# Scaling expert results before they are stored, and adding them to X by accumulating gathers

## The reference

```
scores = softmax(x @ gate_weight.T)              # 8 experts
topk_w, topk_idx = top_k(scores, 2)              # two experts per token, weights not renormalised
combine[t, topk_idx] = topk_w
gu  = einsum('th,efh->tef', x, gate_up_weights)
act = silu(gu[..., :F]) * gu[..., F:]            # F = 352
y   = einsum('tef,te,ehf->th', act, combine, down_weights)
y   = y + shared_ffn(x)
x   = layernorm(x + y)
```

## Time and profile before

| | us |
|---|---|
| median of 3 runs | 2266.09 |
| lowest and highest of them | 2261.15, 2271.64 |
| the profiled execution, device time | 2257.88 |
| its span in the profile, first to last instruction | 2256.1 |
| TensorE busy in the span | 1998.7 (89%) |
| VectorE busy | 1076.1 (48%) |
| ScalarE busy | 712.7 (32%) |
| GpSimd busy | 346.1 (15%) |
| expert phase, about | 1933 to 2256 |

### The profile page before, as it was taken

How to read it: one execution, slowest core, us unless ns; L and a number is a source line. 1 busy time by engine, 2 the same in 40 slices (tenths; PEclk the granted TensorE clock), 3 DMA queues, 4 the chain that set the end, 5 groups by cost and what they waited for, 6 DMA issues and landing times. The chain is left out here.

```text
span 2256.1 us, 32905 instructions
## 1 busy us (share of the span) xinstructions
PE 1998.7 (89%) x12204; PEld 1620.9 (72%) x12204; DVE 1076.1 (48%) x1877; ACT 712.7 (32%) x2272; POOL 346.1 (15%) x308
## 2 busy tenths in 40 slices
PE   5899958899999988999799997898967999899990
PEld 4767736778888857777677875676756777799990
DVE  5566743345454546433454445566765232222226
ACT  1555622334344432222131101344542121233322
POOL 1111100000000018200021100000002400544315
PEclk9999968999999999999899998899988999999995
DMA  5001124000000013000092002000013200444236
GB/s 183 18 22 39 40 105 146 32 1 1 1 1 1 1 43 112 1 0 0 27 335 86 1 1 66 1 1 1 1 42 117 112 0 0 170 164 155 82 102 196
DMA packets 61436, 135.88 MB, mean 60 GB/s; under 512 B 6256, under 2 KB 24048, under 8 KB 59376
## 3 DMA queue, kind: packets, MB, share of 16 engines
q1 hardware_dynamic: 36240, 94.14, 11.9%
q0 software_dynamic: 5840, 27.92, 3.5%
q10 hardware_dynamic: 19216, 11.89, 1.9%
HBM read 90.68 MB, written 43.25 MB: 59 GB/s over the span
## 5 line engine op out<-in xcount | busy, mean ns | idle before, releaser
L1210 PE MATMUL banks<-ternary_xth,ternary_wq 128*128 (+1 forms) x352 | 138.5, 394 | 1.4 <-DVE ternary_xtl L73 1.4
L1210 PE MATMUL banks<-ternary_xtl,ternary_wq 128*128 (+1 forms) x352 | 138.3, 393 | 0.0
L409 ACT ACTIVATE gqa_pr<-banks,gqa_nb 128x128 f32<-128x128 f32 x256 | 90.1, 379 | 60.8 <-DVE gqa_nb L545 60.8
L409 ACT ACTIVATE causal_pr<-banks,causal_nb 128x128 f32<-128x128 f32 x256 | 90.1, 378 | 56.8 <-DVE causal_nb L545 56.8
L100 PE MATMUL banks<-latent_vh,latent_cth 128*128 128x512 f32 x256 | 104.2, 407 | 3.5 <-DVE latent_ctl L923 3.5
L100 PE MATMUL banks<-weights,expert_xgh 128*128 x312 | 104.6, 335 | 2.7 <-DVE expert_xgl L1732 2.4
L101 PE MATMUL banks<-weights,expert_xgh 128*128 x312 | 101.2, 325 | 0.0
L102 PE MATMUL banks<-weights,expert_xgl 128*128 x312 | 101.1, 324 | 0.0
L102 PE MATMUL banks<-latent_vh,latent_ctl 128*128 128x512 f32 x256 | 100.1, 391 | 0.0
L101 PE MATMUL banks<-latent_vl,latent_cth 128*128 128x512 f32 x256 | 100.1, 391 | 0.0
L880 ACT ACTIVATE latent_pt<-banks 128x1024 f32<-128x1024 f32 x32 | 32.9, 1027 | 194.4 <-PE banks L1021 194.4
(11 more groups left out here) (427 smaller groups left out, 5616.1 us busy)
## 6 DMA issues: line engine op xcount, KB each, us to landing
x_slots<-decay_zeros SPq DMA_DIRECT2D x39, 256.0 KB, 3.0
y_slots<-decay_zeros SPq DMA_DIRECT2D x39, 256.0 KB, 3.3
expert_xin<-x_slots SPq DMA_DIRECT2D x39, 256.0 KB, 2.9
y_slots<-expert_ys SPq DMA_DIRECT2D x39, 256.0 KB
weights_raw<-in_expert_experts SPq DMA_DIRECT2D x4, 2176.0 KB, 8.8
gqa_tw<-in_ternary_w ACTq DMA_DIRECT2D x4, 2112.0 KB, 10.9
ternary_raw<-in_ternary_w SPq DMA_DIRECT2D x11, 768.0 KB, 4.2
expert_raw<-in_expert_experts POOLq DMA_DIRECT2D x3, 2176.0 KB, 9.5
```

The lines of the kernel that those rows point to most:

```text
L409: a = act.activation(pr[:, h, c, :], S.bank[2 * h + c // 4][:, (c % 4) * P:(c % 4 + 1) * P], ACT.Exp, bias=nb[:, h, c:c + 1], accum_out=su ...
L1210: a = pe.matmul(dst[:, :], wq[:, j, m, c * P:(c + 1) * P], x[:, c, toks], start=c == 0 and n == 0, stop=c == C - 1 and n == 1)
```

## The change

Four things are done. The decay phase zero-fills a third HBM table `s_slots`, one float per slot. GpSimd, after its 32 scatters of X in the shared phase, scatters the 32 columns of weights to `s_slots` (4 bytes per row) and waits for them. In the expert phase SyncE loads the 128 weights of each slot tile to `sc` (four buffers), and ScalarE's copy out of the bank takes them as a per-partition scale. The gathers no longer write `yg` but add to the tiles of X (`compute_op=ALU.add`); high gather t waits until low gather t has landed, low gathers wait for nothing but `landed(E - 2)`. VectorE's 32 adds are gone; its statistics wait for both gathers of a tile. All five norms stand behind all gathers on GpSimd.

```diff
@@ attention_phase, sync (decay)
-                sp.wait_ge(slots_zero, 32 * (SLOTS // P))
+                sp.dma_start(S.s_slots.rearrange("(p i) n -> p (i n)", p=P), zeros[:, 0:TILES]).then_inc(slots_zero, 16)
+                sp.wait_ge(slots_zero, 32 * (SLOTS // P) + 16)
@@ shared_ffn_phase, gpsimd (after the scatters of X)
+            for n in range(2 * B):
+                at = bass.IndirectOffsetOnAxis(ap=S.pos[:, n:n + 1], axis=0)
+                pool.indirect_dma_start(S.s_slots, at, S.score[:, n:n + 1], None).then_inc(scored, 16)
+            pool.wait_ge(scored, 16 * 2 * B)
@@ expert_ffn_phase
-    NY = 8
-        yg = S.raw[:, 0:NY * DM].rearrange("p (n d) -> p n d", d=DM)
+        sc = sb("sc", [P, NX])
@@ sync
+            def load_score(i):
+                sp.dma_start(sc[:, i % NX:i % NX + 1], rows(S.s_slots, i)).then_inc(s_in[i % NX], 16)
             for i in range(NX):
                 load(i)
+            for i in range(NX):
+                load_score(i)
...
                 sp.dma_start(rows(S.y_slots, i), ys[:, i % 2, :]).then_inc(y_out[i % 2], 16)
+                if i + NX < TILES:
+                    load_score(i + NX)
@@ gpsimd
-                pool.indirect_dma_start(yg[:, n % NY, :], None, S.y_slots, at).then_inc(yg_in[n % NY], 16)
+                pool.indirect_dma_start(S.X[:, n % B, :], None, S.y_slots, at, compute_op=ALU.add).then_inc(added[n % B], 16)
             landed(E - 2)
-            for n in range(B):
-                if n >= NY:
-                    pool.wait_ge(low_added, n - NY + 1)
-                gather(n)
+            for t in range(B):
+                gather(t)
             landed(E - 1)
             for t in range(B):
-                if t < NY:
-                    pool.wait_ge(low_added, t + NY + 1)
-                else:
-                    pool.wait_ge(high_added, t - NY + 1)
+                pool.wait_ge(added[t], 16)
                 gather(B + t)
-                if t >= NY and t % 4 == 3:
-                    norm(t // 4 - 2)
-            for k in range(2, len(sets)):
+            for k in range(len(sets)):
                 norm(k)
@@ scalar
+                act.wait_ge(s_in[i % NX], 16 * (i // NX + 1))
-                act.activation(ys[:, i % 2, :], yb[i % 2], ACT.Copy).then_inc(y_copied, 1)
+                act.activation(ys[:, i % 2, :], yb[i % 2], ACT.Copy, scale=sc[:, i % NX:i % NX + 1]).then_inc(y_copied, 1)
@@ vector (low and high, with their 32 scalar_tensor_tensor, are removed)
             ends = [hi - 1 for lo, hi in sets]
-            for n in range(B + 2):
+            for n in range(B + 1):
                 if n < B:
-                    high(n)
-                if 1 <= n <= B:
-                    dve.wait_ge(high_added, n)
-                    dve.bn_stats(out=six[:, n - 1, :], in_=S.X[:, n - 1, :]).then_inc(six_done, 1)
-                if n >= 2:
-                    dve.wait_ge(six_done, n - 1)
-                    dve.bn_aggr(out=mv[:, n - 2, :], in_=six[:, n - 2, :]).then_inc(mv_done, 1)
-                    if n - 2 in ends:
-                        spread(ends.index(n - 2))
-                if n - 4 in ends:
-                    shifts(ends.index(n - 4))
+                    dve.wait_ge(added[n], 32)
+                    dve.bn_stats(out=six[:, n, :], in_=S.X[:, n, :]).then_inc(six_done, 1)
+                if n >= 1:
+                    dve.wait_ge(six_done, n)
+                    dve.bn_aggr(out=mv[:, n - 1, :], in_=six[:, n - 1, :]).then_inc(mv_done, 1)
+                    if n - 1 in ends:
+                        spread(ends.index(n - 1))
+                if n - 3 in ends:
+                    shifts(ends.index(n - 3))
```

More of the change, by code:

```diff
@@ L1281, in shared_ffn_phase @@
         route_in, given_done, ranked = sem("route_in"), sem("given_done"), sem("ranked")
-        slots_done, rows_done, scattered = sem("slots_done"), sem("rows_done"), sem("scattered")
+        slots_done, rows_done, scattered, scored = sem("slots_done"), sem("rows_done"), sem("scattered"), sem("scored")
         gw_in, gw_zero, gw_hi, gw_lo = sem("gw_in"), sem("gw_zero"), sem("gw_hi"), sem("gw_lo")
@@ L1592, in expert_ffn_phase @@
         y_out = [sem(f"y_out{b}") for b in range(2)]
-        yg_in = [sem(f"yg_in{b}") for b in range(NY)]
+        s_in = [sem(f"s_in{b}") for b in range(NX)]
+        added = [sem(f"added{b}") for b in range(B)]
         w_hi, w_ready, tile_done, spare_set = sem("w_hi"), sem("w_ready"), sem("tile_done"), sem("spare_set")
@@ L1597, in expert_ffn_phase @@
         ht_full, ht_hi, ht_lo = sem("ht_full"), sem("ht_hi"), sem("ht_lo")
-        y_copied, low_added, high_added = sem("y_copied"), sem("low_added"), sem("high_added")
+        y_copied = sem("y_copied")
         six_done, mv_done, ve_done, rs_done = sem("six_done"), sem("mv_done"), sem("ve_done"), sem("rs_done")
@@ L1746, in _ @@
                 dve.tensor_tensor(htl[:, i % 2, :], ht[:, 0:HW], f32(hth[:, i % 2, :]), ALU.subtract).then_inc(ht_lo, 1)
[L1748 to L1759, removed]
             def spread(k):
@@ L1772, in _ @@
             ends = [hi - 1 for lo, hi in sets]
-            for n in range(B + 2):
+            for n in range(B + 1):
                 if n < B:
-                    high(n)
-                if 1 <= n <= B:
-                    dve.wait_ge(high_added, n)
-                    dve.bn_stats(out=six[:, n - 1, :], in_=S.X[:, n - 1, :]).then_inc(six_done, 1)
-                if n >= 2:
-                    dve.wait_ge(six_done, n - 1)
-                    dve.bn_aggr(out=mv[:, n - 2, :], in_=six[:, n - 2, :]).then_inc(mv_done, 1)
-                    if n - 2 in ends:
-                        spread(ends.index(n - 2))
-                if n - 4 in ends:
-                    shifts(ends.index(n - 4))
+                    dve.wait_ge(added[n], 32)
[7 more added lines that the diff above has]
+                    shifts(ends.index(n - 3))
             for k in range(len(sets)):
-                if ends[k] + 4 >= B + 2:
+                if ends[k] + 3 >= B + 1:
                     shifts(k)
@@ L1874, in build @@
         S.landed_at = sb("landed_at", [P, E], U32)
+        S.s_slots = nc.dram_tensor("s_slots", (SLOTS, 1), F32).ap()
         S.ring, S.owner1 = sb("ring", [P, TILES], U32), sb("owner1", [P, TILES], U32)
```

## The result

The changed kernel takes 2269.18 us (median of 20 runs, 2263.03 to 2272.03) against 2263.88 for the kernel before (median of 20, 2258.04 to 2271.64). The ratio is 1.0022, with a 95% interval of 1.0013 to 1.0031: 3 to 7 us slower. The forecast was 2263, 3 us less than the 2266.09 that was known then; the kernel became about 5 us slower, so the sign is wrong and the size about 8 us off. The profiled execution took 2266.12 us (span 2264.3, before 2257.88 and 2256.1).

The account below looks back on a forecast made before the run. The tail's chain of gathers, statistics, normalisations and stores was taken to bound the kernel. Accumulation's -2.5, +0.5 and +0.1 were taken as -3 us: 2263 from 2266.09, range 2255 to 2286.

Parts of the forecast that it names:

- What bounds the kernel: TensorE fills the expert loop; time is decided from GpSimd's low gathers at 2181.6 to the span's end at 2256.1.
- part 1: Low gathers: GpSimd's 12.32 us wait for VectorE's first low add goes; first high gather 4.6 us earlier, at 2210.85.
- Part 3: High gathers: accumulation takes twice the transfer (1.82 us each), same GpSimd issue; gain falls to 2.5 us in place of 6.2.
- part 2: High gathers to end: norms behind all gathers, 16 normalisations in 11.5 us, stores 5.0; at copying price 6.2 us less.
- Rival A: Tail: accumulating gathers are slow at GpSimd's issue; at p = 2.4, 20.5 us more. Chance of p over 2.11: 0.25.
- p: Distance in us between two gathers at GpSimd; Rival A's end is 2199.8 + 32p, which equals 2256.1 at 1.76.
- Part 4: Last expert tiles, 36 to 38: more gathers beside them delay the last result by zero to 2 us, taken as 0.5.
- Part 5: Zero fill, weight scatters, weight loads and scaled copy in earlier phases and loop: hidden, except 0.1 us for the last copy.
- Rival C: Expert loop: late or blocking weight loads make ScalarE wait at each of 39 tiles, 12 us more, 2278; chance 0.02.

Follow-up runs that it names:

- e1: Changed kernel with plain copying gathers that overwrite X instead of adding to it; tail 62.9 us, ratio to the kernel before 0.9944.
- e2: Changed kernel with accumulating gathers of 256 columns in place of 512, half the bytes; tail 78.3 us, ratio to the kernel before 1.0023.
- e3: Changed kernel with the norms of sets 0, 1 and 2 back between the high gathers; tail 77.6 us, ratio to the kernel before 1.0020.
- e5: Kernel before with only the weights' path (zero fill, scatters, loads, scaled copy), VectorE adding without a scale; tail 74.9 us, ratio 1.0110.
- e6: e5 with sixteen gather buffers, the 16 low gathers accumulating in X and the high ones copying; tail 72.2 us, ratio to the kernel before 1.0085.
- e7: e6 with only the first 8 low gathers accumulating, the other 8 copying; tail 66.3 us, ratio to the kernel before 1.0071.
- e8: e5 with GpSimd waiting after every fourth weight scatter until all have landed; tail 74.7 us, ratio to the kernel before 1.0006.
- e9: e5 without its 32 weight scatters and their wait; tail 74.4 us, ratio to the kernel before 1.0008.
- e4: Kernel before with sixteen copying gather buffers in place of eight, none of the weights' path; tail 65.3 us, ratio 0.9963.

## Why the prediction was wrong

**What bounds the kernel, and part 1.** Right in place: the chain goes through gathers, statistics, normalisations and stores, and the wait of 12.3 us is gone. The gain was mis-sized. I let `landed(E - 1)` wait for the second marker ("The last store of results had landed by 2210.34") and kept gathers 1.33 us apart. With copying gathers (e1) GpSimd passes behind the first marker, so that the first high gather comes after 23.88 us in place of the forecast 28.9, and they are 1.25 us apart. The mistake is that I hadn't counted the tiles in use: `landed` waits for their number, and which marker is the last to be needed depends on the data. The edits without the price of the accumulation give 11.3 us on the tail, not "6.2 us less", which I had called the most that they can give.

**Part 3 is the step that failed.** "I take twice the transfer and the same issue." The transfer was right: 1.75 us of the DMA engines per gather against 1.82 forecast. By the Trainium skill ("Collectives: The Full Stack", "The bandwidth ceiling: the fold count and why AG ≠ RS ≠ AR"), whose factor of 1.93 gave an estimated 1.76, the trace agrees. What failed is the same issue: the instruction on GpSimd went from 0.95 to 1.54 us, so that the gathers came 1.84 us apart, not 1.33, and e2 shows that this, not the transfer, sets the pace: half the bytes, same time. The measured value lies between my two ends for the issue, 1.04 and twice that, and I took the lower end, arguing that the same indices are walked. The sum of part 3 also let 11.2 us of output stores run beside the later gathers. They hardly could: the first was issued at 2247.20, behind the last gather's issue, because all norms stand there, as part 2 itself says. From the first high gather to the end it forecast 42.8 us and 48.5 were measured.

**Rival A** had the mechanism and the formula: with p = 1.84 and the later start, 2186.03 + 32 x 1.84 + 17.8 = 2262.7, measured 2264.3. The rest is mostly part 2's "same 5.0 us behind it": 16 stores in one piece need 6.1 us after the last normalisation. I gave A only the part above p = 2.11, since only there it leaves the 0.5%, and let the issue at its lower end decide the sign. With issue halfway between the bounds, p = 1.87, the formula would have said 2259.6 against 2256.1, slower by 3.5. The sign hung on p = 1.76, well inside my own bounds of 1.33 and 2.4. That the time fell inside the stated range is owed to A, which carried its upper end, and not to the forecast's own sum.

**Part 2.** Norms behind all gathers, VectorE standing at `shifts(0)` for 12.5 us, 16 normalisations in 11.8 us: as forecast. The other order that e3 tried gave 0.7 us.

**Part 4.** Not so: tiles 36 to 38 ran without the waits called remote of the earlier trace rows; the last copy out of the bank came 22.7 us after the first low gather, 23.7 before. It was 1 us better, not 0.5 worse.

**Part 5.** In this kernel it was hidden, as forecast, but for the 2.9 us before the shared phase that stay open: from its first to its last Silu that phase takes 188.0 us in both, the loop 81.00 of 81.00, and a scaled copy 0.69 us against the 0.60 of the earlier trace rows. But "they could take 3 times as long before the barrier moved" looked at the barrier only; in e5, e6 and e7 the phase took 23 us more with the same scatters, for a reason that stays open. Rival C named a different place, the loads in the loop; its 12 us are excluded by e8 and e9.

**Sum of the tail**, from e1 and the two profiles: -11.3 for the waits, the moved norms and the removed adds, +9.5 for accumulation in the high gathers, +5.9 for that in the low ones, together +4.1 as measured.

## What to carry to other kernels

An accumulating gather takes an add off VectorE and puts a good half more on GpSimd's issue and nearly twice on the DMA engines; where gathers are the chain and VectorE has room, that is a loss, and more buffers, in memory that was idle by then, remove the same wait without that price (e4). When a copy's price stands in the trace and a variant's doesn't, find the value at which the sign turns before picking one; if it lies between the bounds, the sign is open. And when a queue is filled without a break, read every engine's waits beside it, not only the barrier behind it: in three kernels here engines that never use that queue were held up meanwhile.

## What the runs showed of the hardware that I had not expected

- An accumulating gather of 128 rows: 1.54 us on GpSimd whether the rows have 2 KB or 1 KB, 0.95 for a copy. It moves one row of 2 KB per packet, 128 packets where a copy has 64 of two rows.
- The last store of results, 256 KB to HBM, kept ScalarE's second marker waiting for 1.95 us in e1, where hardly a gather flew beside it, and for 3.80 us in the changed kernel, in the middle of the accumulating ones.
- Thirty-two back-to-back scatters of 128 times 4 bytes, with a DMA share near zero, went together with a stand of 30 us on ScalarE and a crawling TensorE in three of seven kernels that had them. ScalarE's stand ended 4.5 to 4.7 us after the last one's descriptors. All three ran on one chip. The kernel that waits after every fourth scatter didn't stall, on another chip.
